# Two conditioned attention blocks on one core: the keys' exponentials are turned by VectorE and placed by DMAs instead of TensorE; one query tile moves; x3 gets another bank

## What is computed

```python
# block 0: full attention, 16 heads of 32
att = einsum('bnhl,bmhl->bnmh', q, k) + (1 - mask) * -1e6
y   = einsum('bnmh,bmhl->bnhl', softmax(att, axis=2), v)
# block 1: linear attention, 8 heads of 64
q   = softmax(q.reshape(b, t, h, dh), axis=-1)      # over a head's features
k   = softmax(k.reshape(b, t, h, dh), axis=1)       # over the 512 positions
att = einsum('bnhd,bnhl->bhdl', k, v)
y   = einsum('bnhd,bhdl->bnhl', q, att)
```

## Time and profile before

| what | value |
|---|---|
| time, median of 3 | 2653.22 us |
| profiled execution | 2654.44 us, of that 2652.6 us span |
| granted TensorE clock, mean | 0.99 |
| attention_phase | 0 to about 1462 us |
| projection_phase, row 0 with its weights | about 1462 to 1604 us |
| projection_phase, rows of the loop and the last | about 1604 to 2652.6 us |
| TensorE busy | 2591.9 us (98%) |
| VectorE / ScalarE / GpSimd busy | 1817.8 / 1251.5 / 1345.1 us |

### The profile page before, as it was taken

How to read it: one execution, slowest core, us unless ns; L and a number is a source line. 1 busy time by engine, 2 the same in 40 slices (tenths; PEclk the granted TensorE clock), 3 DMA queues, 4 the chain that set the end, 5 groups by cost and what they waited for, 6 DMA issues and landing times. The chain is left out here.

```text
span 2652.6 us, 43842 instructions
## 1 busy us (share of the span) xinstructions
PE 2591.9 (98%) x13634; PEld 1912.1 (72%) x13634; DVE 1817.8 (69%) x3277; ACT 1251.5 (47%) x2097; POOL 1345.1 (51%) x634
## 2 busy tenths in 40 slices
PE   7999999999999999999999789999999999999999
PEld 5666666666666666666663578888888888888887
DVE  6666666666666666666655777777777777777775
ACT  3555556555655566556655323333333333333333
POOL 1666666666666666666664234444343333443343
PEclk9999999999999999999999899999999999999999
DMA  6667666766676667666765411111111111111110
GB/s 146 97 86 108 100 101 85 106 100 101 85 106 101 101 85 106 101 101 85 106 101 152 152 33 53 52 52 52 52 52 49 47 40 43 35 50 52 49 35 32
DMA packets 141027, 211.44 MB, mean 80 GB/s; under 512 B 13944, under 2 KB 48812, under 8 KB 140988
## 3 DMA queue, kind: packets, MB, share of 16 engines
q1 hardware_dynamic: 104124, 143.82, 26.0%
q10 hardware_dynamic: 36864, 67.13, 19.1%
HBM read 74.87 MB, written 34.18 MB: 41 GB/s over the span
## 5 line engine op out<-in xcount | busy, mean ns | idle before, releaser
L809 ACT ACTIVATE probs<-exp_bank 128x512 f32<-128x512 f32 x1024 | 590.0, 598 | 504.2 <-PE exp_bank L553 431.5
L953 DVE TENSOR_REDUCE negmax<-max_bank 128x1 f32<-128x512 f32 x1024 | 680.7, 688 | 207.3 <-PE max_bank L538 205.9
L299 POOL TENSOR_TENSOR probs_sum<-probs_sum,probs 128x2048 f32<-128x2048 f32 x124 | 571.8, 4612 | 29.6 <-ACT probs L809 22.8
L299 POOL TENSOR_TENSOR probs_sum<-probs 128x2048 f32<-128x2048 f32 x63 | 289.4, 4594 | 496.4 <-ACT probs L809 496.4
L553 PE MATMUL exp_bank<-q_stack,k_stack 100*128 100x512 f32 x1024 | 422.3, 421 | 11.3 <-ACT probs L809 11.3
L538 PE MATMUL max_bank<-k_stack,q_stack 98*128 98x512 f32 x1024 | 417.5, 409 | 4.8 <-DVE negmax L953 2.3
L553 PEld LDWEIGHTS exp_bank<-q_stack,k_stack 100*128 100x128 f32 x1024 | 193.0, 189 | 137.8 <-ACT probs L809 52.7
L538 PEld LDWEIGHTS max_bank<-k_stack,q_stack 98*128 98x128 f32 x1024 | 192.8, 189 | 107.2 <-issue 54.5
L1650 POOL TENSOR_TENSOR sT_lo<-silu,sT_hi 128x512 fp32r<-128x512 f32 x124 | 164.9, 1345 | 188.1 <-DVE sT_hi L1798 188.1
L564 PE MATMUL y_bank<-probs,v_sb 128*32 128x512 f32 x2048 | 250.4, 607 | 0.0
L1645 POOL TENSOR_TENSOR rstd_y<-var_eps_y,b_minus_half 128x4 f32<-128x4 f32 x32 | 32.4, 1013 | 363.9 <-DVE var_eps_y L1734 363.9
(11 more groups left out here) (212 smaller groups left out, 5401.2 us busy)
## 6 DMA issues: line engine op xcount, KB each, us to landing
q_stack<-q_stage ACTq DMA_DIRECT2D x128, 256.0 KB
k_stack<-k_stage ACTq DMA_DIRECT2D x128, 256.0 KB
x_sb<-in_x SPq DMA_DIRECT2D x16, 1024.0 KB, 5.7
q_stack<-q_stage SPq DMA_DIRECT2D x64, 256.0 KB
k_stack<-k_stage SPq DMA_DIRECT2D x64, 256.0 KB
yT_scratch<-y_stage SPq DMA_DIRECT2D x64, 256.0 KB, 6.5
area<-yT_scratch SPq DMA_DIRECT2D x64, 256.0 KB, 4.4
area<-in_x SPq DMA_DIRECT2D x64, 256.0 KB, 2.8
```

The costliest lines, as they stand in the source:

```text
L299: eng.tensor_tensor(probs_sum[:, :, :], so_far, probs[:, mt, :, :], ALU.add).then_inc(probs_added, 1)
L809: act.activation(probs[:, mt, j, :], exp_bank[k % 2][:, :], ACT.Exp).then_inc(exp_done, 1)
L953: dve.tensor_reduce(negmax[:, m:m + 1], max_bank[m % 2][:, :], AXX, ALU.max, negate=True).then_inc(max_done, 1)
```

## The change

In `projection_phase`, H and its ScalarE copies are gone. VectorE turns the exponentials in 32x32 blocks (`turn_keys`, four instructions behind the last `k_max`) into `key_blocks`; SP stores those to a scratch tensor in DRAM with four DMAs, waits for them, and loads them with 16 DMAs in pieces of 32 floats to their places (`move_keys`). The loaded keys take the place of `ekT`, the turned blocks that of the former `ek`. ScalarE's silus of L come behind all four exponentials of K. TensorE does queries 0, 1 and 2 before C, and 3 behind it (two and two before). In `attention_phase`, x3 is turned in slot 10 into `max_bank[0]`, its low part made in slot 11, and ScalarE issues the stacking DMAs in slots 4 and 5 (q) and 8 (k) instead of 3 and 7.

```diff
-        X_TURNS = (8, 9, 10, 11)
-        X_LOWS = (8, 10, 11, 12)
+        X_TURNS = (8, 9, 10, 10)
+        X_LOWS = (8, 10, 11, 11)
+        def bank_of_x(tt, static):
+            return max_bank[0] if static >= len(FIRST_USES) and tt == TT - 1 else work_bank[static % 2]
+        HIGH_ISSUES = {"q": {4: slice(0, 1), 5: slice(1, 2)}, "k": {8: slice(0, 2)}}
...
-            def transpose_x(tt, number):
-                out = take_bank(number)
+            def transpose_x(tt, number, beside_maxima=None):
+                if beside_maxima is None:
+                    out = take_bank(number)
+                else:
+                    pe.wait_ge(max_done, beside_maxima)
+                    out = max_bank[0][:, :]
...
                     for what in "qk":
+                        if k in HIGH_ISSUES[what] and (not last or g < NG - 2):
+                            stack_high(what, (g + 2) % NG, high_count(b, g, "qk".index(what)), HIGH_ISSUES[what][k])
                         if k == QUARTERS[what][-1] and (not last or g < NG - 2):
...
                             high_of(what, (g + 2) % NG, number, static)
-                            stack_high(what, (g + 2) % NG, high_count(b, g, "qk".index(what)))
...
-        ekT, ek, v_sb, q_sb = (tiles(area1, i) for i in range(4))
-        eqT = ekT
+        ekT, eqT, v_sb, q_sb = (tiles(area1, i) for i in range(4))
+        key_blocks = area1[:, 1, :].rearrange("p (t c g b) -> p t c g b", t=TT, c=BLOCKS, g=NG)
+        ek = tiles(area1, 0)
...
-        ORDER = (tiles_of("K") + [("-", 0), ("-", 1)] + tiles_of("LVM") + [("-", 2), ("-", 3)] + tiles_of("SH")
-                 + [("Q", 0), ("Q", 1)] + tiles_of("C") + [("Q", 2), ("Q", 3)] + tiles_of("JXY"))
+        ORDER = (tiles_of("KLVM") + [("-", 0), ("-", 1)] + tiles_of("S") + [("Q", 0), ("Q", 1), ("Q", 2)]
+                 + tiles_of("C") + [("Q", 3)] + tiles_of("JXY"))
...
+            def move_keys(b):
+                sp.wait_ge(k_turned, NG * (b + 1))
+                for c in range(BLOCKS):
+                    sp.dma_start(ek_dram[b][c].rearrange("p (t f) -> p t f", t=TT),
+                                 key_blocks[:, :, c, :, :].rearrange("p t g b -> p t (g b)")).then_inc(k_stored, DMA)
+                sp.wait_ge(k_stored, DMA * BLOCKS * (b + 1))
+                for c in range(BLOCKS):
+                    for r in range(BLOCKS):
+                        sp.dma_start(area1[c * BLOCK:(c + 1) * BLOCK, 0, :].rearrange("a (q r b) -> a q r b", r=BLOCKS, b=BLOCK)[:, :, r, :],
+                                     ek_dram[b][c][r * BLOCK:(r + 1) * BLOCK, :].rearrange("a (q b) -> a q b", b=BLOCK)).then_inc(ek_in, DMA)
...
                     load_mask_bias(b + 1)
+                move_keys(b)
+                if kind != "last":
                     if more:
...
             def attention(kind, b):
-                for tt in range(TT):
-                    wait_read(pe, kind, b, "H", tt)
+                pe.wait_ge(ek_in, DMA * BLOCKS * BLOCKS * (b + 1))
                 pe.wait_ge(v_done, TT * (b + 1))
...
-                H(kind, b)
-
-                Q(kind, b, (0, 1))
+                Q(kind, b, (0, 1, 2))
                 if kind != "last":
 
                     C(kind, b, KT * (2 * b + 2))
-                Q(kind, b, (2, 3))
+                Q(kind, b, (3,))
...
+            def turn_keys(b, g):
+                dve.wait_ge(k_exp_done, NG * b + g + 1)
+                dve.transpose(key_blocks[:, :, :, g, :].rearrange("p t c b -> p (t c) b"),
+                              ekT[:, g, :].rearrange("p (q a) -> p q a", a=BLOCK)).then_inc(k_turned, 1)
```

More of the change, by code:

```diff
@@ L733, in step @@
                             project_quarter(what, tile, banks[name], kt, kt == 0, kt == KT - 1)
[L734 to L737, removed]
+                    if g == 1 and not last:
+                        for tt in turned_in(k):
+                            pe.wait_ge(xhat_done, TT * (b + 1) + tt + 1)
+                            transpose_x(tt, use(b, 1, f"x{tt}"),
+                                        SLOTS * (step_of(b, 1) + 2) - 1 if tt == TT - 1 else None)
                     if has_next:
@@ L778, in high_of, with stack_high @@
                                bias=bias[what][:, g:g + 1]).then_inc(hi_done, 1)
-            def stack_high(what, g, highs):
+            def stack_high(what, g, highs, part=slice(0, 2)):
                 act.wait_ge(hi_done, highs)
-                for row in HIGH_ROWS[what]:
+                for row in HIGH_ROWS[what][part]:
                     act.dma_start(stack_rows(what, row, g), stage[what][:, 0, :].bitcast(F32)).then_inc(stack_in[g], DMA)
@@ L869, in step @@
                             high_of(what, (g + 2) % NG, number, static)
-                            stack_high(what, (g + 2) % NG, high_count(b, g, "qk".index(what)))
[L871 to L874, removed]
+                    if g == 1 and not last:
+                        for tt in turned_in(k):
+                            static, number = use(b, 1, f"x{tt}")
+                            high_of_x(tt, number, static)
                     if g == 1 and not last and 5 <= k < 5 + TT:
@@ L1071, in step @@
                             low_of(what, (g + 2) % NG, use(b, g, what, last)[0], high_count(b, g, i))
-                    if g == 1 and not last and k in X_LOWS:
-                        tt = X_LOWS.index(k)
-                        low_of_x(tt, use(b, 1, f"x{tt}")[0], high_count(b, 1, 2 + tt))
+                    for tt in range(TT):
+                        if g == 1 and not last and k == X_LOWS[tt]:
+                            low_of_x(tt, use(b, 1, f"x{tt}")[0], high_count(b, 1, 2 + tt))
                     if g == 0 and not last and k == 11:
@@ L1564, in last_iteration @@
                 V("last", b, range(TT))
-                H("last", b)
                 Q("last", b, range(TT))
@@ L1618, in iteration @@
                 if kind != "first":
-                    silus(kind, b, "L", 1, b - 1, KT * 2 * b, range(KT - 1, KT))
+                    silus(kind, b, "L", 1, b - 1, KT * 2 * b)
                 for tt in range(TT):
@@ L1692, in iteration @@
                 for tt in range(TT):
-                    if tt == 2 and kind != "last":
+                    if tt == TT - 1 and kind != "last":
                         inverse_deviation("x1", b + 1)
@@ L1899, in iteration @@
                     low_of_w("out1")
+                    dve.wait_ge(w_split["out1"], 1)
                     dve.wait_ge(bias_done, 3)
-                else:
+                for g in range(NG):
+                    turn_keys(b, g)
+                if kind != "first":
                     highs_of_silu(kind, b, "L")
```

29 lines of the change are left out of this document (13 added, 16 removed).

## The result

The changed kernel takes 2678.83 us (median of 4 runs, 2676.85 to 2679.98), the kernel before 2653.48 us beside it. The ratio is 1.0094 with a 95% interval of 1.0079 to 1.0108: slower by 25 us, where 39 us less were forecast, and above the range of 2603 to 2664 us. Its profiled execution took 2678.9 us.

What follows compares the result with a forecast made beforehand. TensorE's own work was taken to bound each loop row, at 71.14 us. Profiled 2654.44 - 27.9 (H) + 2.8 (row 0's transposes) - 14 (attention) = 2615.3 us; median forecast 2614 us, range 2603 to 2664 us.

Steps and rivals of the forecast that it cites:

- H: Loop rows: TensorE's transposes of the keys, half of a 3.49 us piece; removal saves 1.745 us in 16 rows, 27.9 us.
- x3: Attention phase: copying x3 a slot earlier halves TensorE's 0.60 us wait for an exponential, 0.3 us in 15 rows, 4.5 us.
- Then SP issues 16 loads at the spacing of its loads of y, 1.84 / 4 = 0.46 us: SP's list in loop rows: the key loads take 7.4 us to issue, so y is late by 1.4 us only.
- a slack of 3.3: Loop rows, ahead of C: the result's stores may land 3.3 us later than before without cost.
- issues of SP of 0.6 us: Small-price rival on SP's list: 9.6 us of issues, y 3.6 us late; 2614 to 2640 us; chance 0.20.
- 0.8 or more: Sign in the profile after: the 16 loads on SP spaced 0.8 us or more apart means their packets hold them back.
- the first rival: SP's list: y and result's stores queue behind key loads, delaying GpSimd, then C; 48 us at 25.4 ns, 2662 us; chance 0.20.
- the cases at 25.4 and 51 ns: Key-load packets at the 512 B price, 2662 us (slower by packets, chance 0.20), or double, about 2830 us (chance 0.05).
- The attention phase: Attention rows: spreading ScalarE's issues and moving x3 saves 14 us, taken between 16.9 and 11.3 us.
- the issues of q and k: Attention phase: ScalarE's two q issues cost TensorE 0.20 us in 62 of 64 steps; spreading them over slots saves 12.4 us.
- VectorE's transposes: Loop rows: four key transposes, 2.8 us, end at 2095.6 in a row starting at 2079.91, off the chain.
- 2.2 us behind the low parts: Loop rows: with a third query tile ahead, C starts 2.2 us after GpSimd's last low part of S.

## Why the prediction was wrong

- **The step that failed**: "Then SP issues 16 loads at the spacing of its loads of y, 1.84 / 4 = 0.46 us". It was 0.73 us, since each issue takes 0.575 instead of 0.33 us. That is 11.7 us where 7.4 stood, and with the keys' stores 0.8 us later, y was issued 6.9 us later than before, not 1.4. With the stores then queued behind y's data, they landed 7.0 us late against a slack of 3.3: a wait of 3.7 us by the prediction's own slack, 3.2 measured. The price had been taken from the DMA that was nearest by engine. A dear one stood in the earlier trace rows, 1.21 us for two issues, and the forecast used it for ScalarE alone. Its rival of "issues of SP of 0.6 us" was priced at "0.3 us too much": 0.6 us is about what one issue took, but from one issue to the next it was 0.15 us more. Its sign for slow packets, a spacing of "0.8 or more", could hardly have told them from dear issues either, which alone gave 0.73 us.
- **What the sum left out**: the granted clock. Behind waits of about 3.2 us the next 11 us of matmuls became 1.9 us longer in 9 of 13 rows, 17 us of the loss. The forecast priced a wait by its length alone.
- **The rival of the same place and another cause**: SP's list did make C wait, as the first rival had it, but not by packets. They took 12.7 ns, inside the 10 to 15 taken, and the cases at 25.4 and 51 ns fall. The estimate of 51 ns for a small packet was worked out from the Trainium skill's rule of at least 512 B for line rate ("DMA: Bandwidth & Descriptors", Specifications). The trace disagrees with the estimate: 12.7 ns is half of the 25.4 ns of a 512 B packet, which was a store where this is a load. As to the rate it agrees with the rule: 128 B in 12.7 ns are 10 bytes per ns, 512 B in 25.4 ns are 20. The same page of the Trainium skill, in its account of a fixed overhead (section "Why small descriptors are slow"), gave an estimate of 9.4 ns, which is nearer.
- **H**: 25.5 us lie between the attention edits alone (2643.98) and the changed kernel with its loads behind the stores (2618.47). 27.9 - 2.5 (row 0's wait grew from 9.9 to 12.4 us, 2.8 forecast) = 25.4 us. Both terms held.
- **The attention phase**: 10.4 us, not 14. x3 gave 3.2 (4.5 counted), the issues of q and k about 7 where 9.5 remained of the 14. The direction held and the size was off. How it splits is less sure: x3's share lies between 0 and 5 us, the other is a difference of two runs, and TensorE's waits show only 11.3 - 7.5 = 3.8 us of the whole.
- **VectorE's transposes**: the stores of the keys went out 2034.02 - 2018.31 = 15.7 us behind the row's keys, as forecast (2095.6 - 2079.91).
- **Slack and the third tile**: "2.2 us behind the low parts" came out with the loads behind the stores. There the low parts end at 1749.50 + 4.09 = 1753.59, and C starts three tiles behind 1747.59, at 1755.77: 2.2 us. The third tile covers what it was said to.
- With these sizes the forecast's 2614 becomes 2614 + 3.6 (attention) - 0.3 (row 0) = 2617.3 us for a kernel whose SP list is in order (2618.3 and 2618.5 measured), and with the 60.3 us of waits and clock 2677.6 us for the changed one (2678.8 measured).

## What to carry to other kernels

Before DMAs are put on an engine's list, price each by the spacing of a DMA that is cut in the same way, and add the sum to everything that stands behind; where nothing like it is in the trace, measure the issue first. Put DMAs with slack behind those that free a buffer: here the same 16 loads cost 60 us ahead of four stores and nothing behind them. And price a wait of TensorE with the clock that may fall behind it.

## What the hardware showed

- SP needed 0.315 us to issue a load that is one stretch per partition, and 0.56 to 0.575 us for the same bytes cut into 4 pieces on the partition, or into 16 on the partition or in DRAM. From one issue to the next it was 0.48 and 0.73 us.
- ScalarE issued the cut loads no faster: 0.572 us was its median issue too, and the 16 took 13.71 us, where SP took 11.7.
- A 128 B packet from DRAM took 12.7 ns of an engine, and 16 loads kept the engines only 56% busy.
- The granted clock of C behind a wait of TensorE: 1.00 after waits of 0.4 to 0.9 us; after 3.0 to 4.3 us 0.87 in 9 rows and 1.00 in four; 0.82 after 5.9 us and 0.90 after 5.8 us, over 60 matmuls instead of 48.
